# The second layer's three-token convolution: as three taps after the projection, or as three products inside it

## The reference

```
xz = einsum('bld,ed->ble', u, in_w);  xm, z = split(xz, 2)
xc = conv1d(xm, c1_w, causal, 3 tokens, one filter per channel)
xm = silu(xc + c1_b)
dbl = einsum('bld,ed->ble', xm, xp_w)            # dt_r, B (16 states), C (16 states)
dt = softplus(dt_r @ dt_w.T + dt_b)
h = exp(dt * A) * h + (dt * xm) * B              # per token, channel and state
y = (sum over states of h * C + xm * D) * silu(z)
out = y @ out_w.T
```

## Time and profile before

| what | value |
|---|---|
| median of 3 runs | 1646.45 us (1641.7 to 1650.43) |
| span of the profiled execution | 1644.6 us |
| busy over the span: PE, DVE, ACT, POOL | 1289.1, 1293.9, 1163.7, 971.4 us |
| mean granted TensorE clock | 0.786 of full |
| the mixer stage, first instruction to first scan | 721.7 to 773.17 us |
| the mixer stage, last output of VectorE | 1500.26 us |
| scans (1796), 384 of them | 463.9 us on DVE |
| multiplications by C (1807), 128 | 221.6 us on DVE |
| drives (1417), 128 | 438.5 us on POOL |

### The profile page before, as it was taken

How to read it: one execution, slowest core, us unless ns; L and a number is a source line. 1 busy time by engine, 2 the same in 40 slices (tenths; PEclk the granted TensorE clock), 3 DMA queues, 4 the chain that set the end, 5 groups by cost and what they waited for, 6 DMA issues and landing times. The chain is left out here.

```text
span 1644.6 us, 15347 instructions
## 1 busy us (share of the span) xinstructions
PE 1289.1 (78%) x3822; PEld 436.0 (27%) x3822; DVE 1293.9 (79%) x1306; ACT 1163.7 (71%) x1787; POOL 971.4 (59%) x515
## 2 busy tenths in 40 slices
PE   4999766685862777767888898888898888775995
PEld 2344201110100455532222222222222222111563
DVE  1655569999995577711999999999999999994675
ACT  2676368687772577748888988888889888740564
POOL 2400038969697323315898888898888898860000
PEclk8999855555555899978788988888878988655998
DMA  5344460200003133317777777777777776734573
GB/s 155 101 139 130 107 171 0 96 6 13 38 1 109 44 96 96 88 51 169 171 165 160 182 178 175 173 170 173 174 176 174 168 168 145 163 79 101 122 174 75
DMA packets 136423, 200.44 MB, mean 122 GB/s; under 512 B 26739, under 2 KB 68770, under 8 KB 135564
## 3 DMA queue, kind: packets, MB, share of 16 engines
q1 hardware_dynamic: 133740, 196.15, 49.2%
q10 hardware_dynamic: 2160, 2.61, 0.6%
q0 software_dynamic: 448, 0.85, 0.2%
HBM read 145.93 MB, written 53.63 MB: 121 GB/s over the span
## 5 line engine op out<-in xcount | busy, mean ns | idle before, releaser
L1796 DVE TENSOR_TENSOR_SCAN m_h<-m_qa,m_state,m_ub 128x512 f32<-128x512 f32 x384 | 463.9, 1261 | 16.0 <-POOL m_ub L1417 11.6
L1417 POOL TENSOR_TENSOR m_ub<-m_dlb,m_bt 128x1536 f32<-128x1536 f32 x128 | 438.5, 3445 | 16.4 <-DVE m_h L1796 11.4
L1757 ACT ACTIVATE m_qa<-m_dlb,k_a 128x512 f32<-128x512 f32 x384 | 254.2, 682 | 89.3 <-DVE m_h L1796 88.0
L1137 POOL TENSOR_TENSOR b_u<-b_dl,b_z 128x1024 f32<-128x1024 f32 x48 | 125.3, 2610 | 210.9 <-DVE b_dl L1054 210.4
L1610 PE MATMUL m_qc<-m_bcr,k_selc 32*128 32x512 f32 x256 | 167.2, 737 | 99.2 <-DVE m_g L1807 99.0
L1807 DVE TENSOR_TENSOR m_g<-m_h,m_qc 128x1536 f32<-128x1536 f32 x128 | 221.6, 1731 | 11.9 <-issue 6.6
L1627 PE MATMUL m_qy<-m_g,k_seld 128*32 128x512 f32 x768 | 175.1, 767 | 0.0
L984 PE MATMUL b_qb<-b_bc,k_pack_sel 96*128 96x512 bf16 x96 | 81.6, 850 | 73.2 <-DVE b_u L1060 71.0
L1551 PE MATMUL m_qf<-m_cva,k_conv 113*96 113x504 f32 (+1 forms) x192 | 105.0, 689 | 5.0 <-PEq L1171 5.0
L1610 PEld LDWEIGHTS m_qc<-m_bcr,k_selc 32*128 32x128 f32 x256 | 42.7, 208 | 223.2 <-issue 187.2
L1023 ACT ACTIVATE b_qa<-b_dl,b_a 128x1024 f32<-128x1024 f32 x48 | 53.7, 1118 | 61.8 <-DVE b_dl L1054 61.8
(11 more groups left out here) (187 smaller groups left out, 2645.3 us busy)
## 6 DMA issues: line engine op xcount, KB each, us to landing
m_dlb<-scratch_dldu SPq DMA_DIRECT2D x128, 384.0 KB, 10.3
m_bt<-scratch_brow SPq DMA_DIRECT2D x128, 256.0 KB, 5.9
scratch_dldu<-m_dldu SPq DMA_DIRECT2D x32, 384.0 KB, 3.2
scratch_z<-a_z SPq DMA_DIRECT2D x24, 256.0 KB, 6.0
b_z<-scratch_z SPq DMA_DIRECT2D x3, 2048.0 KB, 11.1
scratch_y<-b_yrow SPq DMA_DIRECT2D x12, 512.0 KB, 2.6
c_y<-scratch_y SPq DMA_DIRECT2D x16, 384.0 KB, 3.3
scratch_gate<-m_gt SPq DMA_DIRECT2D x32, 192.0 KB, 3.6
```

The source lines that it names most:

```text
L1137: nc.gpsimd.tensor_tensor(by_column(u[s][:], col), by_column(dl[s][:], col), seen(z[j % 2][:], col, piece), ALU.mult).then_inc(u_ready, 1)
L1417: nc.gpsimd.tensor_tensor(ub[k % 3][:], dlb[u % 2][:, J:2 * J, :], bcast(bt[u % 2][:, n, :], J), ALU.mult).then_inc(ub_ready, 1)
L1757: nc.scalar.activation(q_a[:, j, :], dlb[u % 2][:, j, :], ACT.Exp, scale=G["a1"][:, j, n:n + 1]).then_inc(da, 1)
L1796: nc.vector.tensor_tensor_scan(h[k % 3][:, j, :], q_a[:, j, :], ub[k % 3][:, j, :], state[:, k % NS, j:j + 1], ALU.mult, ALU.add).then_inc ...
```

## The change

The three-token filter is multiplied into the projection's weights, `u_taps[:, k, :]` = projection weights times the filter's column k, made once in front0: POOL builds three more diagonals, PE three more rows, VectorE one product of 96x288. In the mixer stage `xa` takes over the two leading columns and the five buffers of `u1`; PE accumulates three products on the shifted views of `xa` in `q_m`; ScalarE copies the result into `acc`. The taps and POOL's additions are gone, and so are their semaphores. The tail is now copied from `xa` one turn ahead, and the z projection reads `xa` from column 2.

```diff
 pool_shape:   for k in range(3):
                 nc.gpsimd.tensor_scalar(self.diag[:, k, :], R["ident"][0:DI, 0:DI], G["c1_low"][:, k:k + 1], None, ALU.mult)
+                nc.gpsimd.tensor_scalar(self.diag[:, 3 + k, :], R["ident"][0:DI, 0:DI], G["l1_c1w"][:, k:k + 1], None, ALU.mult)
 pe_bias:      for k in range(3):
...
+                self.nc.tensor.matmul(self.ps_low[0:DI, k, P:P + DI], self.ones[:, 0:DI], self.diag[:, 3 + k, :], start=True, stop=True)
 dve_make:
+              nc.vector.tensor_tensor(G["u_taps"][:], bcast(G["l1_min_x"][:], 3), self.ps_low[0:DI, :, P:P + DI], ALU.mult)
 mid1_phase:
-    u1 = [m.sb(f"m_u{r}", [DI, 2 + CH]) for r in range(HIST)]
-    tp = [m.sb(f"m_tp{k}", [DI, CH]) for k in range(3)]
+    xa = [m.sb(f"m_xa{r}", [DI, 2 + CH]) for r in range(HIST)]
 POOL:
-                nc.gpsimd.tensor_tensor(acc[:], tp[0][:], tp[1][:], ALU.add).then_inc(summed, 1)
-                pool.wait_ge(summed, 2 * v + 1)
-                nc.gpsimd.tensor_tensor(acc[:], acc[:], tp[2][:], ALU.add).then_inc(summed, 1)
 PE, u_of(v):
+                if v >= 4:
+                    pe.wait_ge(tail, v - 3)
                 if v >= 1:
                     pe.wait_ge(sz_ready, v)
-                nc.tensor.matmul(q_m[:], G["l1_min_x"][:], xa[v % 2][:], start=True, stop=True).then_inc(u_mm, 1)
+                for k in range(3):
+                    last = nc.tensor.matmul(q_m[:], G["u_taps"][:, k, :], xa[v % HIST][:, k:k + CH], start=(k == 0), stop=(k == 2))
+                last.then_inc(u_mm, 1)
 ACT, window:
-                    act.wait_ge(summed, 2 * b + 2)
+                    act.wait_ge(u_out, b + 1)
 ACT, tail_of(t + 5) in step 2, ahead of u_of(t + 4):
+                nc.scalar.activation(xa[v % HIST][:, 0:2], xa[(v - 4) % HIST][:, CH:CH + 2], ACT.Identity).then_inc(tail, 1)
 ACT, u_of(v):
                 act.wait_ge(u_mm, v + 1)
                 if v >= 1:
+                    act.wait_ge(xm_ready, v)
-                nc.scalar.activation(u1[r][:, 2:2 + CH], q_m[:], ACT.Identity).then_inc(u_out, 1)
+                nc.scalar.activation(acc[:], q_m[:], ACT.Identity).then_inc(u_out, 1)
 ACT, taps(v) in step 0:
-                for k in range(3):
-                    nc.scalar.activation(tp[k][:], u1[v % HIST][:, k:k + CH], ACT.Identity, scale=G["l1_c1w"][:, k:k + 1])
```

More of the change, by code:

```diff
@@ L219, in pool_shape @@
                                     ALU.mult).then_inc(self.shaped, 1)
-        pool.wait_ge(self.shaped, 4)
+            nc.gpsimd.tensor_scalar(self.diag[:, 3 + k, :], R["ident"][0:DI, 0:DI], G["l1_c1w"][:, k:k + 1], None,
+                                    ALU.mult).then_inc(self.shaped, 1)
+        pool.wait_ge(self.shaped, 7)
         nc.gpsimd.memset(G["minus1"][:], -1.0).then_inc(self.shaped, 1)
-        pool.wait_ge(self.shaped, 5)
+        pool.wait_ge(self.shaped, 8)
         nc.gpsimd.tensor_copy(G["selc"][DI:P], R["ident"][DI:P, DI:DI + NS].unsqueeze(2).broadcast_to([32, NS, 32])).then_inc(self.shaped, 1)
@@ L1350, in mid1_phase @@
         cva, cvb, cv_first = G["cva"], G["cvb"], G["cv_first"]
-        xa, gt, yo = ([m.sb(f"m_{n}{r}", [DI, CH]) for r in range(2)] for n in ("xa", "gt", "yo"))
-        u1 = [m.sb(f"m_u{r}", [DI, 2 + CH]) for r in range(HIST)]
-        tp = [m.sb(f"m_tp{k}", [DI, CH]) for k in range(3)]
+        gt, yo = ([m.sb(f"m_{n}{r}", [DI, CH]) for r in range(2)] for n in ("gt", "yo"))
+        xa = [m.sb(f"m_xa{r}", [DI, 2 + CH]) for r in range(HIST)]
         acc = m.sb("m_acc", [DI, CH])
@@ L1369, in mid1_phase @@
         (zeroed, conv_mm, gate_mm, z_mm, u_mm, dt_mm, skip_mm, c_mm, added,
-         xa_ready, gt_ready, sz_ready, xm_ready, tail, u_out, taps_out, bc_out, soft, da, kept,
-         summed, corr, du_ready, ub_ready, delta, scanned, read, y_ready) = (
+         xa_ready, gt_ready, sz_ready, xm_ready, tail, u_out, bc_out, soft, da, kept,
+         corr, du_ready, ub_ready, delta, scanned, read, y_ready) = (
             m.sem(f"m_{n}") for n in (
                 "zeroed", "conv_mm", "gate_mm", "z_mm", "u_mm", "dt_mm", "skip_mm", "c_mm", "added",
-                "xa_ready", "gt_ready", "sz_ready", "xm_ready", "tail", "u_out", "taps_out", "bc_out", "soft", "da", "kept",
-                "summed", "corr", "du_ready", "ub_ready", "delta", "scanned", "read", "y_ready"))
+                "xa_ready", "gt_ready", "sz_ready", "xm_ready", "tail", "u_out", "bc_out", "soft", "da", "kept",
+                "corr", "du_ready", "ub_ready", "delta", "scanned", "read", "y_ready"))
         cv_loaded, gt_stored, dldu_stored, dlb_loaded, bt_loaded, y_stored = (
@@ L1580, in z_of @@
                 pe.wait_ge(u_out, v + 1)
-                nc.tensor.matmul(q_m[:], G["l1_min_z"][:], xa[v % 2][:], start=True, stop=True).then_inc(z_mm, 1)
+                nc.tensor.matmul(q_m[:], G["l1_min_z"][:], xa[v % HIST][:, 2:2 + CH], start=True, stop=True).then_inc(z_mm, 1)
             def u_of(v):
@@ L1586, in u_of @@
                 pe.wait_ge(xa_ready, v + 1)
+                if v == 0:
+                    pe.wait_ge(zeroed, NZ)
+                if v >= 4:
+                    pe.wait_ge(tail, v - 3)
                 if v >= 1:
                     pe.wait_ge(sz_ready, v)
-                nc.tensor.matmul(q_m[:], G["l1_min_x"][:], xa[v % 2][:], start=True, stop=True).then_inc(u_mm, 1)
+                for k in range(3):
+                    last = nc.tensor.matmul(q_m[:], G["u_taps"][:, k, :], xa[v % HIST][:, k:k + CH], start=(k == 0),
+                                            stop=(k == 2))
+                last.then_inc(u_mm, 1)
             def dt_of(v):
@@ L1656, in window @@
                     act.wait_ge(conv_mm, a + 1)
[L1658 to L1661, removed]
+                    if a >= HIST:
+                        act.wait_ge(z_mm, a - HIST + 1)
+                        act.wait_ge(u_mm, a - HIST + 1)
+                        act.wait_ge(tail, a - HIST + 1)
+                    nc.scalar.activation(xa[a % HIST][:, 2:2 + CH], q_f[:], ACT.Silu).then_inc(xa_ready, 1)
                     act.wait_ge(gate_mm, a + 1)
@@ L1679, in window, with tail_of @@
                 act.preload_act_table_set(LOG_EXP_SET)
+            def tail_of(v):
+                if not exists(v) or v < 4:
+                    return
+                act.wait_ge(xa_ready, v - 3)
+                if v == 4:
+                    act.wait_ge(zeroed, NZ)
+                if v >= HIST:
+                    act.wait_ge(u_mm, v - HIST + 1)
+                nc.scalar.activation(xa[v % HIST][:, 0:2], xa[(v - 4) % HIST][:, CH:CH + 2], ACT.Identity).then_inc(tail, 1)
             def u_of(v):
@@ L1771, in step @@
                 if s == 2:
+                    tail_of(t + 5)
                     u_of(t + 4)
@@ L1777, in step @@
                     rows_out(t + 2)
-                    taps(t + 3)
             turns(step)
```

46 lines of the change are left out of this document (11 added, 35 removed).

## The result

The changed kernel takes 1696.41 us (median of 4 runs, 1692.17 to 1697.74) against 1645.89 us (1641.7 to 1650.43, 4 runs) before: ratio 1.0294 [1.0264, 1.0324], slower by 50 us. The forecast was 1658.5, so the sign was right and the size four times too small.

The account below looks back on a forecast made before the run. VectorE was taken as the bound. Steady run 6, start 5 and weights 1 sum to +12 us on the median of 1646.45, giving 1658.5 us; the range for 8 in 10 was 1640 to 1673.

Parts of the forecast that it names:

- Bound: Second layer's state-space stage: VectorE is the bound, with only 12.3 of 600 us idle in the stretch 800 to 1400 us.
- What goes: Per unit, three ScalarE taps and two POOL additions go, off the path; only 2.7 us of decay waits would end.
- Start: Stage's beginning up to the first scans, run in series with the new products on the path: +5 us, 0 to +9.
- the 1.7 of my first sum: Start: 1.7 us added by each unit's projection at full clock, making the first softplus 3.1 us later.
- the upper case I had named: Start: two more projections run at half clock, so the first scan's delay could be 5.3 us; 4 was taken.
- Weights: Weights' preparation: six more small TensorE products, a VectorE product and three POOL diagonals, +1 us, 0 to 1.5.
- Steady run: The stage's repeating turns: a loss of +6 us taken, between 12 gained and 12 lost.
- 13 mixed turns: Of 27 turns, about 13 start the projection at half clock and regain full clock: 0.4 us lost each, 5 us.
- four at half clock throughout: Four of the 27 turns stay at half clock: VectorE's waits of 2.4 us become 4.8 in each, +10 us.
- the 2.7 us per turn that I had worked out: TensorE time added per unit by four more instructions at 57% half clock, equal to its idle time before the C broadcast.
- Rival 1: The added TensorE work keeps its clock up, so steady-run stalls go: -12 + 5 + 1 = -6, 1640 us; chance 0.31.
- Rival 2: TensorE becomes each turn's bound, 23.0 us needed, 0.8 above the turn: +28 in all, 1674 us; chance 0.14.

Follow-up runs that it names:

- after_one: The changed kernel with one of the three products, leaving two of the filter's taps out of the result: 1650.78 us, 1.0016.
- after_filler: The changed kernel plus two products (four instructions) per turn that nothing reads, in TensorE's idle spot of step 1: 1646.69 us, 0.9994.
- after_moved: The changed kernel reordered: three products at the end of step 3, z product in step 1, ScalarE's copy in step 0: 1647.26 us, 0.9996.
- after_two: The changed kernel with two of the three products, the oldest token's left out: 1725.86 us, 1.0482.
- after_late: The changed kernel plus two products per turn that nothing reads, at the end of step 3 behind the adding up: 1648.89 us, 1.0017.
- before_three: The kernel before with its projection issued three times, taps and additions kept: 1692.75 us, 1.0280.
- two_filler: The changed kernel with two of the three products, plus two products that nothing reads in step 1: 1642.88 us, 0.9974.
- after_behind: The changed kernel with the three products issued in step 2 behind the dt product, C broadcast and adding up: 1840.33 us, 1.1181.

## Why the prediction was right or wrong

**Bound.** Right: VectorE sets the run, and what it loses is what others make it wait.

**What goes.** Right: the decay waits ended and nothing else came back (after_one). One thing was overlooked: ScalarE's copy keeps its place in step 2 and now waits 61.1 us for longer products [L1700 above], and the softplus behind it comes 0.3 us late in each of the 25 turns. That is 7.8 of the 45.5 us; with the projection at full clock it is 0.6 (after_filler).

**Start.** +5 forecast, +6.3 measured, within 0 to 9. The three projections took 4.48, 5.41 and 5.41 us where the trace before has 1.07, 1.99 and 1.99 (738.12, 750.60 and 764.85 us), so each added 3.4 us, the price at half clock, and not the 1.7 of my first sum: nearer to the upper case I had named. after_moved, where the products stand behind the convolution, has the short start again.

**Weights.** +1 forecast; the wait is 0.5 longer and the new product takes 0.43 us, +0.9. The other 2.6 us of the shift ahead of the stage are not explained by these; of them 1.5 were there before any changed work (166.64 against 165.13 for the same addition). The same point of the stage lay between 719.7 and 725.8 us in the kernels tried, so I take the rest for variation between executions.

**Steady run: the step that failed.** I took +6 us, between -12 and +12; it was +40. What failed is the price of the added work turn by turn. I sorted the old turns by their clock, let each keep the clock that it had, and took 0.4 us for each of 13 mixed turns, 2.4 for each of four at half clock throughout and nothing for the rest; then I let the new work only shrink the half clock, since it fills "one of the idle spots of a turn, just behind the dt product". The new order made it worse. The idle spot that survived is the one directly ahead of step 1's broadcast, the clock fell in it or just behind it in every turn, and all projections ran wholly or partly at half clock (5.44, 4.00 and 4.09 us, against 2.82 for the six at full clock in after_filler). In two of every three turns VectorE lost time, 3.08 and 1.34 us.

The rows show the sum that takes its place. From the start of step 1's broadcast to the end of step 2's, PE needs 6.7 us at full clock, and VectorE is ready 8.5 us after that start: a spare of 1.8 us with the three products in place, where I had 0.1 (1.8 - 1.7). At full clock the products cost next to nothing in the stretch (after_filler). Half clock makes the 6.7 us into 8.4, 9.8 and 11.6, so PE comes 1.7, 3.1 and 4.8 us later; less the spare, that is 0, 1.3 and 3.0 us, the waits seen. With 0.31 for the softplus in each turn that makes 5.3 us in three turns, 1.8 per turn against 0.46 before (12.3/27).

An average would have served better here. Before, the same way from broadcast to broadcast took 7.1 us on average in the 27 turns of the stretch, and VectorE was ready for the second 1.6 us after its end; the mean of the new three is 9.9, so the change added 2.8, close to the 2.7 us per turn that I had worked out. An estimate from these averages is 27 x (2.7 - 1.6) = 30 us in the stretch, against 33 (45.5 - 12.3) measured, 7.8 of them the softplus. I had the 2.7 and went on with smaller prices. It is luck in part, since an average holds only where no turn has much spare left over.

**Rival 1** (the clock stays up) did not come by itself; but with the fillers it came, and its price was right in kind: in after_filler the run lost nothing and gained 9 us, against the 12 I gave it. **Rival 2** priced PE as too slow by 0.8 us per turn on average. That isn't the mechanism either, since PE was idle 55.7 us and another 54 us of fillers fit in. Its ground for disbelief, that "a PE without idle time is not seen at half clock for long", is refuted: in after_two PE was busy 10.0 of 10.0 us from 1025 to 1035 at a granted 0.50.

The Trainium skill, page "TensorE: Matmul & The Clock Gate", section "Part 1: The HAM clock gate", has activity release the throttle. The row just named doesn't agree for a busy engine as such (10.0 of 10.0 us, and 0.50); the fillers agree in that two more products per turn went with 0.95 and 0.96. Its section "HAM oscillation — how this bites in real kernels" tells of a loop in which each pass waits and so starts slow again; that half clock stood behind 25 of 25 idle spots of the changed kernel agrees, that it stood behind 15 of 27 in after_late agrees only in part.

**What stays open.** Why a stretch lasts 3.5 us in one case and 7, 10 or nearly 14 in another, and why two products lock into the longest. A reading that fits the rows: PE's late broadcast of step 2 stalls VectorE, PE then works through the rest of the turn without a pause, and so all its idle time gathers in one spot in step 1 (25 spots of 2.23 us are all of the 55.7), behind which the clock is halved for the next step 2. All 25 spots in one place, against 36 in three places before, speak for it. It isn't the whole rule, and the length of the spot isn't either: spots of 1.40 us were followed by half clock 24 times of 24 in after_two, spots of 1.37 us 3 times of 15 in after_late. That the loss is the clock in step 2 is shown (before_three, after_filler, two_filler); how the clock chooses is not.

## What to carry to other kernels

When an engine shares a loop with the one that sets the time, price added work by where it stands, between the engine's idle spot and the next thing that the bound waits for, and not by the engine's room per turn: here four instructions cost 46 us in one step and nothing in another. If TensorE's granted clock is below full, take both clock levels for the whole new piece and every turn as an end of the range, and try filler products outside the urgent step; they are no gain by themselves, for in the kernel before they raised the clock from 0.86 to 0.95 and left the time as it was. When moving a producer, look where its consumer stands in the other engine's queue: in after_behind the copy that stayed held up the decays behind it.

## What the runs showed of the hardware that was not expected

TensorE's time was not monotone in its work: one, two and three products per unit gave 1650.8, 1725.9 and 1696.4 us, with granted clocks of 0.85, 0.74 and 0.86 in the steady run. Products that nothing reads, four instructions and 2 us per turn, raised the clock from 0.86 to 0.95 or 0.96 and took 41 to 50 us off in the three places tried. Idle spots of 2.2 us were followed by half clock 25 times of 25 in the changed kernel, 16 of 16 in the kernel before, 12 of 12 in after_late and 24 of 25 in before_three; spots of 1.40 us 24 times of 24 in after_two, and spots of nearly the same length, 1.37 us, only 3 times of 15 in after_late.
